# The last gathered table of 1000 rows becomes a one-hot table

## The chip, the cores and the metric

One core of one Trainium2 chip. The metric is device microseconds of one execution of the program; the median of several timed runs is given. Engines: TensorE (PE, with its weight loads shown apart as PEld), VectorE (DVE), ScalarE (ACT), GpSimd (POOL), SyncE (SP).

## What is computed

A recommendation model's interaction and top layers, for 2048 samples. Each sample has 27 ids; id f picks a row of 128 fp32 numbers from table f. Twelve tables have 1000 rows, the others 1250, 12,500 or 125,000.

```python
e = stack([tbl_f[ids[:, f]] for f in range(27)], axis=1)   # (2048, 27, 128)
inter = einsum('bfd,bgd->bfg', e, e).reshape(2048, 27 * 27)
x = inter[:, lower_triangle_without_diagonal]              # 351 pairs
h = concatenate([bottom, x, bottom], axis=1)               # (2048, 607)
h = maximum(h @ W_top1 + b_top1, 0)                        # 512
h = maximum(h @ W_top2 + b_top2, 0)                        # 256
y = h @ W_top3                                             # (2048, 1)
```

## The kernel before

The batch is worked in 8 halves of 256 samples (`HALVES`), each of two tiles of 128. Halves 0, 1 and 7 are written out, 2 to 6 are a loop on each engine. The code is written by hand for every engine, with counting semaphores.

**Two ways to a row.** `slots` divides the tables: the first `ONEHOT_TABLES` (11) with 1000 rows are one-hot, the other 16 are gathered; the slots of the gathered ones come first. A gathered table is fetched by `gather` on GpSimd: one indirect DMA (line 393) per slot and tile of 128 samples, 32 in a half, into `rows`. The rows are transposed on TensorE by `transpose_tile` (line 740), four slots to a PSUM bank: `TQ` = 4 such uses per tile, `FQ` = 4 slots each. ScalarE copies the bank into `embT` (`emb_tile`, line 548). Before a half overwrites `rows`, GpSimd waits until TensorE has transposed those of the half before.

A one-hot table lies in SBUF whole, as a high part (fp32 rounded to fp32r) and a low part (the rest), in 8 blocks of 125 rows (`VB`, `VP`). For 256 samples VectorE builds, for each block, a matrix of 125 x 256 that is 1 where the row is the sample's id (`make_hot`, line 433), and TensorE multiplies each block's high and low part with it and sums all 16 products in one bank (`onehot_unit`, line 728). Two tables share a unit and a bank; the matmuls of a table are 125x256, the hot matrices of a unit 125x512. With 11 tables there are six units, and the last has one table. A unit has four parts (two blocks each); VectorE may be four parts ahead of TensorE (`HOT_SLOTS`). It makes a part when the slot's last user is through. ScalarE copies a finished unit out (`emb_hot`, line 541).

**The order.** TensorE and ScalarE follow one list:

```python
plan = ([("hot", 0), ("hot", 1), ("tile", 0, 0), ("hot", 2), ("tile", 0, 1), ("hot", 3), ("tile", 0, 2), ("hot", 4),
         ("tile", 0, 3), ("hot", 5)] + [("tile", 1, u) for u in range(TQ)])
```

The two build banks (`ps_build`) serve units 0, 2, 4 and 1, 3, 5 in turn, then the row uses of tile 1: its first waits for the copy of unit 4, its second for the copy of unit 5. Behind the first two uses of tile 1 stand the pair products of tile 0 (`pair_products`, line 754: 64 products of two samples each, recorded as 128 matmuls of 52 columns), then the dense layers of the half before (lines 774, 802, 810) with the last two row uses between, then the pair products of tile 1. The products go by DVE and ACT copies to `gram`, to DRAM and back as `pairX`, whose 351 pair rows feed the next half's first layer. The last half multiplies per sample (line 766), and rearranges its pairs with transposes on TensorE (lines 821, 832) in the tail.

**Tables in the first half.** SP loads each one-hot table (500 KB) into one of five raw slots (`RAWS`, `load_table`); from the sixth on it waits until VectorE has made the low part of the table five before. ScalarE makes the high part (`split_table`, line 522), VectorE the low part (line 408). VectorE's order in the first half is, for each unit: its four hot parts, then the low parts of its tables. TensorE starts a unit when these are there. ScalarE's order is written out by hand: high parts of the next tables stand between its copies; `load_weights` (1.74 MB from ScalarE's queue) stands behind table 9. Behind the last table SP issues the first bottom rows and the ids of the next half.

Of the kernel before, what the change touches and what calls it, by code (L numbers as in the profile page):

```python
# [3 lines left out]

BATCH, FEATURES, D = 2048, 27, 128
SMALL_VOCAB = 1000
ONEHOT_TABLES = 11
HALF, TILE = 256, 128
HALVES = BATCH // HALF
FIRST, LAST = 0, HALVES - 1  # L10
# [17 lines left out]
def slots(vocabs):  # L28

    onehot = [f for f in range(FEATURES) if vocabs[f] == SMALL_VOCAB][:ONEHOT_TABLES]  # L30
    gathered = [f for f in range(FEATURES) if f not in onehot]
# [25 lines left out]
def dlrm_tower(nc, bottom, ids, ids_onehot, tables, w_bottom_a, w_pairs, w_bottom_b, b1, w2, b2, w3, scratch, out):  # L57
# [10 lines left out]
    TQ = (NG + FQ - 1) // FQ  # L68
# [19 lines left out]
    def bank_slots(u):  # L88

        return range(u * FQ, min((u + 1) * FQ, NG))  # L90

    def nth(*use):
        return plan.index(use)
# [46 lines left out]
    with ctx:  # L140
        def sb(name, shape, dt):
            return ctx.enter_context(nc.sbuf_tensor(name, shape, dt))
# [42 lines left out]
        ident = sb("ident", [128, 128], fp32)  # L185
# [65 lines left out]
        def build_at(s):  # L251
            return (ps_build + gram_banks)[banks[s]]
# [259 lines left out]
        def _(act):  # L512
# [7 lines left out]
            def split_table(q):  # L520
                act.wait_ge(raw_in[q % RAWS], 32 * (q // RAWS + 1))
                nc.scalar.copy(table[0:VP, q, HIGH, :], raw[0:VP, q % RAWS, :]).then_inc(table_high, 1)
# [12 lines left out]
            def emb_hot(i, p):  # L535
                s = nth("hot", p)
                act.wait_ge(built, BUILDS * i + s + 1)
                n = len(units[p])
                src = build_at(s)[:, 0:n * HALF].rearrange("p (q b) -> p b q", q=n)
                f = NG + units[p][0]  # L540
                nc.scalar.copy(embT[:, :, f:f + n], src).then_inc(emb_done, 1)  # L541

            def emb_tile(i, t, u):
                s = nth("tile", t, u)
                n = len(bank_slots(u))
                act.wait_ge(built, BUILDS * i + s + 1)
                src = build_at(s)[:, 0:n * 128].rearrange("p (f b) -> p b f", f=n)
                nc.scalar.copy(embT[:, t * TILE:(t + 1) * TILE, u * FQ:u * FQ + n], src).then_inc(emb_done, 1)  # L548
# [103 lines left out]
            emb_hot(FIRST, 3)  # L652
            emb_tile(FIRST, 0, 2)
            split_table(10)
            emb_hot(FIRST, 4)
            emb_tile(FIRST, 0, 3)
            emb_hot(FIRST, 5)
# [24 lines left out]
        def _(pe):  # L682
# [32 lines left out]
            def onehot_unit(i, n):  # L715

                s = nth("hot", n)
                bank = build_bank(i, s)
                for a in parts_of(n):
                    v0 = parts[a][1]  # L720
                    if is_half(i, FIRST) and v0 == 0:
                        pe.wait_ge(table_low, units[n][-1] + 1)
                    pe.wait_ge(hot_made, HOTS * i + a + 1)
                    for q in range(len(units[n])):
                        for v in range(VS):
                            row = (v0 + v) * D
                            for bits in (HIGH, LOW):
                                last = nc.tensor.matmul(bank[:, q * HALF:(q + 1) * HALF],  # L728
                                                        table[0:VP, units[n][q], bits, row:row + D],
                                                        hot[0:VP, a % HOT_SLOTS, v, q, :],  # L730
                                                        start=(v0 == v == q == bits == 0),
                                                        stop=(v0 == VB - VS and v == VS - 1 and bits == LOW),
                                                        skip_group_check=True)
                    last.then_inc(built if ends_unit(a) else hot_used, 1)

            def transpose_tile(i, t, u):
                pe.wait_ge(rows_in[t][u], 16 * len(bank_slots(u)) * (i + 1))
                bank = build_bank(i, nth("tile", t, u))
                for f, s in enumerate(bank_slots(u)):
                    last = nc.tensor.transpose(bank[:, f * 128:(f + 1) * 128], rows[:, t, s * D:(s + 1) * D], ident[:, :])  # L740
                last.then_inc(built, 1)
# [94 lines left out]
            def features(i):  # L836
                for use in plan[0:BUILDS - TQ + EARLY]:
                    if use[0] == "hot":
                        onehot_unit(i, use[1])
                    else:  # L840
                        transpose_tile(i, use[1], use[2])

            def first_tile(i):
                if is_half(i, LAST):
                    end_products(0)
                else:
                    pair_products(i, 0)
# [27 lines left out]
                second_tile(i)  # L875

            pe.wait_ge(consts_made, 3)
            features(FIRST)
            first_tile(FIRST)
            second_rows(FIRST)  # L880
# [61 lines left out]
```

## Time and profile before

| | us |
|---|---|
| timed runs, median of 3 | 408.24 (406.95 to 410.33) |
| profiled execution, span from first to last instruction | 600.9 |
| PE, matmuls busy in it | 416.6 |
| POOL busy | 253.9 |
| DVE busy | 198.2 |
| ACT busy | 143.3 |

For the profiled execution the profile gives only its span. The profiled execution is far longer than the timed runs, so a reader should not take shares of the span for shares of the timed run, and should look for where the extra time sits. Busy times of matmuls overlap: the distance from one start to the next is what a stream of them costs. The mean granted clock of TensorE in the execution is 0.835 of full speed.

### The profile page before, as it was taken

How to read it: one execution, taken by the hardware profiler on the slowest of the kernel's cores; microseconds unless marked ns; L12 is line 12 of the kernel's file. 1: busy time of each engine (PE TensorE's matmuls, PEld its weight loads, DVE VectorE, ACT ScalarE, POOL GpSimd, SP SyncE). 2: the span in 40 equal slices, each digit the busy share in tenths (PEclk: the TensorE clock that was granted, in tenths of full speed). 3: DMA queues.
4: the chain of work that ended last, by engine and by line, in shares of the span. 5: the costliest groups of instructions: out<-in, count | busy, mean ns of one | idle time of the engine just before them, and what ended most of it. 6: DMA issues, size and time to landing. Idle time of an engine off the chain costs nothing.

```text
span 600.9 us, 11581 instructions
## 1 busy us (share of the span) xinstructions
PE 416.6 (69%) x4550; PEld 378.3 (63%) x4550; DVE 198.2 (33%) x523; ACT 143.3 (24%) x256; POOL 253.9 (42%) x263
## 2 busy tenths in 40 slices
PE   0444655786498836897298955899378972979888
PEld 0434644676388836697186944788276962979766
DVE  3405612265204612074013722065022730138111
ACT  2302321124031221224022230322122230312423
POOL 6773563256440671526622563406723365220000
PEclk9975887698597976999579985989578995889989
DMA  7964721236112461144312461124311362122000
GB/s 161 236 146 108 191 60 52 59 76 107 36 50 54 94 104 42 36 81 92 84 36 53 88 108 31 52 59 93 96 41 31 95 92 70 41 59 52 11 2 1
DMA packets 50590, 44.79 MB, mean 75 GB/s; under 512 B 30211, under 2 KB 43019, under 8 KB 50562
## 3 DMA queue, kind: packets, MB, share of 16 engines
q1 hardware_dynamic: 40746, 25.82, 22.2%
q0 software_dynamic: 8192, 16.79, 10.8%
q10 hardware_dynamic: 1623, 1.79, 1.2%
q8 instruction: 19, 0.31, 0.2%
q14 instruction: 10, 0.07, 0.0%
HBM read 39.52 MB, written 4.85 MB: 74 GB/s over the span
## 4 chain that ended last, share of the span: by engine, by line
PE 63%; issue 23%; another core or an unknown queue 5%; DVE 4%; ACT 2%; DMA 1%; SPq 1%; ACTq 0%; DVEq 0%
PE ps_build L728 26%; PE ps_gram L754 16%; PE ps_dense L774 8%; PE ps_dense L802 4%; PE ps_build L740 3%; DVE hot L433 2%; PE ps_gram L740 2%; DMA raw<-tbl_dram 1%; PE ps_dense L810 1%; PE ps_gram L774 1%; DVE table L408 1%; ACT embT L541 1%; PE ps_gram L766 1%; PE ps_gram L821 1%
## 5 line engine op out<-in xcount | busy, mean ns | idle before, releaser
L393 POOL DMA_INDIRECT rows<-tbl_dram,idx x256 | 253.1, 989 | 275.6 <-PE ps_gram L740 96.2
L728 PE MATMUL ps_build<-hot,table 125*128 125x256 f32 x1408 | 196.3, 299 | 60.1 <-DVE table L408 34.0
L728 PEld LDWEIGHTS ps_build<-hot,table 125*128 125x128 f32 x1408 | 184.9, 204 | 65.6 <-issue 53.8
L754 PE MATMUL ps_gram<-embT 128*53 128x52 f32 x1792 | 99.5, 254 | 107.2 <-issue 106.5
L754 PEld LDWEIGHTS ps_gram<-embT 128*53 128x53 f32 x1792 | 80.8, 166 | 127.9 <-issue 125.4
L433 DVE TENSOR_SCALAR hot<-id_raw 125x512 fp32r<-125x512 f32 (+1 forms) x384 | 133.8, 408 | 76.4 <-remote 33.3
L446 DVE COPY gram<-ps_gram 117x416 f32<-117x416 f32 x28 | 16.6, 592 | 229.8 <-remote 151.1
L541 ACT COPY embT<-ps_build 128x512 f32<-128x512 f32 (+1 forms) x48 | 37.7, 786 | 176.9 <-PE ps_build L728 82.8
L559 ACT COPY gram<-ps_gram 117x416 f32<-117x416 f32 x28 | 14.2, 506 | 178.7 <-PE ps_gram L754 130.1
L774 PE MATMUL ps_dense<-pairT,w1p 120*128 120x256 f32 (+1 forms) x252 | 37.1, 295 | 0.0
L774 PEld LDWEIGHTS ps_dense<-pairT,w1p 120*128 120x128 f32 (+1 forms) x252 | 34.9, 206 | 0.0
L740 PE MATMUL ps_build<-ident,rows 128*128 128x128 f32 x128 | 20.4, 286 | 8.8 <-issue 6.9
L802 PE MATMUL ps_dense<-h,w2s 128*128 128x256 f32 x112 | 25.3, 379 | 0.0
L423 DVE TENSOR_SCALAR id_raw<-id_raw,vocab 125x512 f32<-125x512 int32 (+1 forms) x48 | 22.2, 462 | 6.2 <-DMA id_raw<-ids_onehot_dram 6.2
L548 ACT COPY embT<-ps_build 128x512 f32<-128x512 f32 x32 | 21.4, 669 | 7.4 <-PE ps_build L740 4.9
L548 ACT COPY embT<-ps_gram 128x512 f32<-128x512 f32 x32 | 21.6, 675 | 4.2 <-DVE w1b L408 2.2
L740 PEld LDWEIGHTS ps_build<-ident,rows 128*128 128x128 f32 x128 | 15.4, 146 | 11.4 <-issue 10.6
L802 PEld LDWEIGHTS ps_dense<-h,w2s 128*128 128x128 f32 x112 | 20.8, 190 | 2.6
L579 ACT ACTIVATE h<-ps_dense,b1s 128x256 f32<-128x256 f32 x28 | 13.3, 473 | 30.6 <-PE ps_dense L774 30.6
L408 DVE TENSOR_TENSOR pairT<-pairX,pairT 120x256 fp32r<-120x256 f32 (+1 forms) x21 | 7.7, 421 | 36.0 <-issue 18.9
L740 PE MATMUL ps_gram<-ident,rows 128*128 128x128 f32 x128 | 19.3, 272 | 0.0
L774 PE MATMUL ps_dense<-botT,w1b 128*128 128x256 f32 x84 | 17.6, 323 | 0.0
(57 smaller groups left out, 147.6 us busy)
## 6 DMA issues: line engine op xcount, KB each, us to landing
id_raw<-ids_onehot_dram SPq DMA_DIRECT2D x40, 256.0 KB
raw<-tbl_dram SPq DMA_DIRECT2D x11, 448.0 KB
gram_dram<-gram SPq DMA_DIRECT2D x56, 84.5 KB
rows<-tbl_dram,idx POOLq DMA_INDIRECT x256
id_raw<-ids_onehot_dram SPq DMA_DIRECT2D x8, 128.0 KB
bot<-bottom_dram SPq DMA_DIRECT2D x8, 128.0 KB
w1p_raw<-w_pairs_dram ACTq DMA_DIRECT2D x1, 720.0 KB
raw<-tbl_dram SPq DMA_DIRECT2D x11, 52.0 KB
```

What stands on the lines that cost most here:

```text
L393: nc.gpsimd.indirect_dma_start(rows[:, t, s * D:(s + 1) * D], None, tables[f], bass.IndirectOffsetOnAxis(idx[:, 2 * i + t, f:f + 1], 0)).t ...
L423: nc.vector.tensor_scalar(shifted, id_raw[0:VP, n % ID_SLOTS, 0:w, :], vocab[0:VP, 0:1], None, ALU.subtract).then_inc(id_shifted, 1)
L433: last = nc.vector.tensor_scalar(hot[0:VP, a % HOT_SLOTS, v, 0:w, :], shifted, float(v0 + v), None, ALU.is_equal)
L446: nc.vector.tensor_copy(*gram_piece(t, 2 * n + 0)).then_inc(gram_dve, 1)
L541: nc.scalar.copy(embT[:, :, f:f + n], src).then_inc(emb_done, 1)
L548: nc.scalar.copy(embT[:, t * TILE:(t + 1) * TILE, u * FQ:u * FQ + n], src).then_inc(emb_done, 1)
L559: nc.scalar.copy(*gram_piece(t, 2 * n + 1)).then_inc(gram_act, 1)
L728: last = nc.tensor.matmul(bank[:, q * HALF:(q + 1) * HALF], table[0:VP, units[n][q], bits, row:row + D], hot[0:VP, a % HOT_SLOTS, v, q, :] ...
L740: last = nc.tensor.transpose(bank[:, f * 128:(f + 1) * 128], rows[:, t, s * D:(s + 1) * D], ident[:, :])
L754: last = nc.tensor.matmul(gram_banks[b][STRIP * q:STRIP * q + GM - STRIP, g * DUO * PG:(g + 1) * DUO * PG], x.rearrange("p k g -> p (k g)" ...
L774: last = nc.tensor.matmul(bank, w(a), x(b), start=(first and m == 0), stop=(end and m == 2))
L802: last = nc.tensor.matmul(bank[:, 0:HALF], w2s[:, c, cols], h1[:, c, :], start=(c == 0), stop=(c == M1 - 1))
```

## The change

`ONEHOT_TABLES` becomes 12. So the twelfth table of 1000 rows is loaded and split like the other eleven, unit 5 has two tables, and 15 tables are gathered: the fourth row use of each tile has three slots. Sizes that follow from the numbers of tables (`NG`, `NO`: the rows, the resident tables, the ids loaded for unit 5) change with them, and SP's loop over tables has one load more, which waits for table 6's low part. ScalarE splits table 11 behind table 10. As the fourth bank of the products is now filled to column 384 only by the transposes, TensorE writes its last 128 columns once, at the start.

```diff
-ONEHOT_TABLES = 11
+ONEHOT_TABLES = 12
...
             emb_tile(FIRST, 0, 2)
             split_table(10)
+            split_table(11)
             emb_hot(FIRST, 4)
...
             pe.wait_ge(consts_made, 3)
+
+            short = TQ - 1
+            nc.tensor.transpose(build_at(nth("tile", 0, short))[:, len(bank_slots(short)) * 128:512], ident[:, :], ident[:, :])
             features(FIRST)
```

## Rows read from the trace of the kernel before

**Rows 1.** The page, part 1: busy time, share of span, instructions.

```profile
PE 416.6 (69%) x4550; PEld 378.3 (63%) x4550; DVE 198.2 (33%) x523; ACT 143.3 (24%) x256; POOL 253.9 (42%) x263
```

**Rows 2.** Windows: length, busy (x) of PE/PEld/DVE/ACT/POOL, clock, DMA share, GB/s.

```profile
324.53:351.70 27.17, 24.88 (x203) 23.88 (x200) 17.32 (x50) 8.39 (x13) 11.50 (x12) 1.00 0.45 89
351.70:374.00 22.30, 9.28 (x129) 6.95 (x128) 2.89 (x7) 2.21 (x6) 11.97 (x13) 0.57 0.31 64
...
580.95:600.90 19.95, 16.99 (x106) 14.35 (x106) 3.55 (x18) 6.16 (x23) 0.00 (x0) 0.84 0.00 1
```

**Rows 3.** Groups by line and shape: count | busy, mean ns | idle before.

```profile
L728 PE MATMUL ps_build<-hot,table 125*128 125x256 f32 x1408 | 196.3, 299 | 60.1 <-DVE table L408 34.0 <-issue 17.1 <-DVE hot L433 7.6
...
L754 PE MATMUL ps_gram<-embT 128*53 128x52 f32 x1792 | 99.5, 254 | 107.2 <-issue 106.5 <-ACT embT L548 0.7
L541 ACT COPY embT<-ps_build 128x512 f32<-128x512 f32 x40 | 32.4, 811 | 163.3 <-PE ps_build L728 76.9 <-remote 52.3 <-PE ps_gram L740 24.4
...
L541 ACT COPY embT<-ps_build 128x256 f32<-128x256 f32 x8 | 5.3, 665 | 13.6 <-PE ps_build L728 5.9 <-PE ps_build L740 4.3 <-remote 3.4
L766 PE MATMUL ps_gram<-embT 128*26 128x26 f32 x512 | 5.1, 192 | 4.6 <-issue 4.6
```

**Rows 4.** PE in order of time, a middle half: start, us, what, idle before.

```profile
337.20 0.60 PE L740 MATMUL ps_gram<-ident,rows 128*128 128x128 f32 x4
337.56 4.08 PE L728 MATMUL ps_build<-hot,table 125*128 125x256 f32 x32
341.47 0.60 PE L740 MATMUL ps_gram<-ident,rows 128*128 128x128 f32 x4
...
347.56 2.15 PE L728 MATMUL ps_build<-hot,table 125*128 125x256 f32 x16
...
379.47 0.52 PE L774 MATMUL ps_dense<-botT,w1b 128*128 128x256 f32 x3
...
380.91 3.62 PE L802 MATMUL ps_dense<-h,w2s 128*128 128x256 f32 x16
384.36 0.60 PE L740 MATMUL ps_build<-ident,rows 128*128 128x128 f32 x4
384.89 1.02 PE L810 MATMUL ps_dense<-h,w3s 128*1 128x256 f32 x4
...
391.68 2.38 PE L754 MATMUL ps_gram<-embT 128*53 128x52 f32 x61 [0.46 <-issue]
393.99 0.58 PE L728 MATMUL ps_build<-hot,table 125*128 125x256 f32 x1
...
559.05 0.63 PE L740 MATMUL ps_build<-ident,rows 128*128 128x128 f32 x4 [0.41 <-ACT embT L541]
```

**Rows 5.** POOL in order of time, the same half.

```profile
334.54 1.10 POOL L393 DMA_INDIRECT rows<-tbl_dram,idx  x1 [12.73 <-PE ps_gram L740]
...
366.38 0.94 POOL L393 DMA_INDIRECT rows<-tbl_dram,idx  x1 [0.30 <-issue]
```

**Rows 6.** The first half: the chain's DMA, then PE and DVE in order of time.

```profile
5.04 9.00 DMA raw<-tbl_dram
...
16.47 5.80 PE L728 MATMUL ps_build<-hot,table 125*128 125x256 f32 x32 [16.47 <-DVE table L408]
...
70.03 5.55 PE L728 MATMUL ps_build<-hot,table 125*128 125x256 f32 x32 [2.73 <-issue]
...
77.35 2.14 PE L728 MATMUL ps_build<-hot,table 125*128 125x256 f32 x16 [1.33 <-ACT embT L548]
...
59.66 0.76 DVE L433 TENSOR_SCALAR hot<-id_raw 125x512 fp32r<-125x512 f32 x2 [0.19 <-PE ps_build L728]
60.34 2.35 DVE L408 TENSOR_TENSOR table<-raw,table 125x1024 fp32r<-125x1024 f32 x2
...
75.62 0.49 DVE L433 TENSOR_SCALAR hot<-id_raw 125x256 fp32r<-125x256 f32 x2 [0.86 <-PE ps_build L728]
76.03 1.22 DVE L408 TENSOR_TENSOR table<-raw,table 125x1024 fp32r<-125x1024 f32 x1
```

## The prediction

> **What bounds the kernel now.** I began with the page: TensorE (PE) is the busiest engine, 416.6 us in a span of 600.9 us [rows 1]. But the span of the profiled execution is 192.7 us above the median of the timed runs, 408.24 us, and its matmul busy time alone is above that median. So the profiled execution holds time that a timed run does not, and shares of its span say little. Where is it? The windows of one half in the middle of the loop show it: its one-hot stage lasts 27.17 us with PE busy for 24.88, and the pair products behind it last 22.30 us with PE busy for 9.28 [rows 2]. The group of the pair products puts its idle time down to "issue", 106.5 us in all, so it waits for nothing that the profile names. In a stretch where the same matmuls run freely, 61 of them start within 2.31 us (391.68 to 393.99), 0.0379 us each, and the 128 of a stage would take 4.9 us instead of 22.3 [rows 3, 4].
>
> So I rebuilt a timed run from start-to-start spacings in undisturbed stretches [rows 4], times the counts [rows 3]:
> - one-hot matmuls: 32 between 337.56 and the transposes at 341.47, 3.91 us; 1408 of them are 44 such sets, 172.0 us;
> - pair products: 1792 x 0.0379 = 67.9 us;
> - transposes: 4 from 337.20 to 337.56, 0.36 us; 256 are 23.0 us;
> - first dense layer: 12 from 379.47 to 380.91, 1.44 us; it has 48 matmuls per half, so 46.1 us over 8 halves. The second layer: 3.45 us per half (380.91 to 384.36), 27.6 us; the third, busy 1.02 us per half, 8.2 us.
>
> That is 344.8 us. The last half's own products are 5.1 us [rows 3], and its tail keeps PE busy for 16.99 us, 10.2 of them its dense layers, which are in the sum: 6.8 more [rows 2]. The first matmul starts at 16.47 us [rows 6]. Together 373.2 us, out of 408.2. The 35.0 us left are waits: in the first half PE stands before each further one-hot unit for its tables' splits, 2.73 us before unit 4 [rows 6], which for five units makes 13.7 us; in the tail 3.0 us of 19.95 [rows 2]; and 18.3 us remain for eight halves, 2.3 us each. A middle half is 5.5 x 3.91 + 8 x 0.36 + 256 x 0.0379 + 5.76 + 3.45 + 1.02 = 44.3 us of matmuls, about 46.6 us with such waits. **PE's throughput sets the end**, nearly without slack.
>
> POOL is the second candidate. A gather is busy 0.94 us behind a gap of 0.30 (366.38), so the 32 of a half take 39.7 us; beside the hot building one is busy 1.10 us (334.54), and 8 such make it 41.0 us [rows 5]. That is 3 us under PE's 44.3 us, and the first gather of a half is preceded by 12.73 us of waiting for PE's transposes (less in a timed run, whose pair products don't stall, but by the sums some 3 us more than nothing). POOL waits for PE.
>
> **The change part by part.**
>
> *Added: 16 matmuls in unit 5 of each half.* Unit 5 has 16 now, busy 2.15 us (347.56); the full unit at 337.56 is busy 4.08 us. Added: 1.93 us per half [rows 4]. They are in PE's only stream, nothing lies beside them. The lower bound is nothing (all of it in waits that PE has today), the upper is the lower clock, by unit 4 of the first half: 5.55 us for 32, 2.8 us for 16 [rows 6]. I take 1.93. The Trainium skill (TensorE: Matmul & The Clock Gate, Back-to-back issue gap and LDWEIGHTS) has two rules here: an isolated matmul of N columns every N/2.4 + 2.5 ns, 109 ns for 256 columns, and a weight load of 107 ns for 128 columns. The 122 ns of a pair in the trace [rows 4] fit a weight load that is hidden and a small cost above the first rule; if the load were not hidden the 128 added pairs would cost 27.6 us, by the first rule alone 14.0 us, by the trace 15.4 us.
>
> *Removed: 2 transposes per half* (the fourth row use of either tile has three slots): 2 x 0.09 = 0.18 us per half, from PE's stream [rows 4].
>
> *Removed: 2 gathers per half on POOL*, 2.5 us of its queue [rows 5]. Worth nothing, as POOL waits for PE; the bounds are 0 and -2.5 us.
>
> *ScalarE.* The copy of unit 5 out of PSUM goes from 128x256, 665 ns, to 128x512, 811 ns: +0.15 us [rows 3]. This one is on the path: the second of the two early transposes writes unit 5's bank, and PE stands 0.41 us before it for this copy (line 541) at 559.05 [rows 4]. I add 0.15 per half. The two copies of the short tiles get narrower; I take nothing for them (at most 0.1 us each).
>
> *VectorE.* A part of unit 5 is two instructions, 0.49 us together for one table (75.62) and 0.76 us for two (59.66) [rows 6]: four parts make +1.1 us per half. VectorE is busy for 17.32 us of the 27.17 of the one-hot stage, so this is hidden [rows 2]. The cover is the four hot slots: a part of unit 5 will need 1.0 us of PE and 0.76 us of VectorE [rows 4, 6]. Without that cover it would be the 1.1 us per half.
>
> A half thus costs 1.93 - 0.18 + 0.15 = +1.90 us, seven halves +13.3 us.
>
> *The first half* is limited otherwise. VectorE makes a unit's last hot part only when PE has freed a slot, and splits the unit's tables behind it. So PE stands still for 2.73 us before unit 4. Before unit 5 the chain is: last hot part 75.62, split 76.03 (1.22 us), PE 77.35 [rows 6]. With two tables the hot part is 0.27 us longer and the splits take 2.35 us, as at 60.34, instead of 1.22: +1.13. So PE starts 1.40 us later, then has 1.93 us more, less 0.18, plus 0.15: **+3.3 us**. At the slower clock that unit 4 shows (5.55 us busy instead of 4.08) the added matmuls are 0.9 us more.
>
> The twelfth table must also land. It is the seventh load that waits for a raw slot, the one of table 6, which is free when its low part is made, at about 61.5 (the first of the two splits of 60.34 to 62.69). A table that was on the path took 9.00 us from issue to landing among a full load [rows 6]: 70.5. ScalarE must split it before its copy of unit 4, due at 75.6. Its split takes about as long as VectorE's, 1.2 us. That leaves 4 us of cover, some 2.5 us if unit 4 runs at full clock, and the weights (1.74 MB) are issued at the same time. I take nothing, and keep +4 us as the upper bound. SP's next loads (the bottom rows and three sets of ids of the next half) stand behind its new wait for the slot; they are wanted a half later, tens of us. The first gathers get 2 fewer and the ids of unit 5 twice 128 KB, both small.
>
> *The one new transpose at the start* runs when the identity is made, in PE's 16.47 us without work: nothing.
>
> Sum: 13.3 + 3.3 = 16.6 us. The durations are those of the profiled execution, its undisturbed stretches; against its own span, 600.9 us, the same sum gives 617.5 us. On the median of the timed runs it is 408.24 + 16.6 = **424.8 us**, 4.1% more.
>
> **The rivals.**
>
> *The added matmuls fill waits that PE has anyway.* For it: some 18 us of the 408 remain as waits by my sum, and the fractions per half (0.41 us before the second early transpose) may be larger than I see. Against: the added matmuls are in unit 5, where PE's stream in the trace has no wait, and hots or gathered rows come no earlier by the change. Then only the first half grows: 411.5 us. Chance 0.07.
>
> *POOL sets the pace, and loses 2 of its 32 gathers.* This is the case on the other side. If a gather took 46.6/32 = 1.46 us in a timed run, POOL would fill the whole half and PE would wait for rows at its transposes. After the change 30 gathers take 43.7 us. Whether that shows depends on PE: from a stream of 44.3 + 1.9 = 46.2 us PE takes over at once, and the time is 408.24 - 7 x 0.4 + 3.3 = 409 us. It decides for a gain where PE's own stream is at least 2.5 us per half shorter than my sum of it; then a half falls by 2.9 us, and 408.24 - 7 x 2.9 + 3.3 = 391 us. For it: gathers beside hot building take 1.40 us with the gap. Against: only 8 of 32 do, the rest 1.24 us, and PE releases the first [rows 5]. The Trainium skill (DMA: Bandwidth & Descriptors, SWDGE vs HWDGE vs iDMA) says that VectorE, in its two-port mode, locks GpSimd out of the memory its descriptors go to; that would raise just these. Chance 0.03 for 409 us and 0.03 for 391 us.
>
> *The twelfth table lands late*, behind the weights: +4 us on top, 428.8 us. Chance 0.10.
>
> *The added matmuls run at 1.2 GHz everywhere.* 8 x 0.9 us more: 432 us. The granted clock was 1.00 over the one-hot stage of the half [rows 2], so I give it 0.03.
>
> **How the numbers follow.** The forecast, 424.8 us with its own range 419 to 428, has 0.73; 0.01 is left for what I do not see. The range: 415 us (half of the addition is absorbed) to 430 us (a late table). The first two rivals and the clock lie outside it, 0.16 together. A difference of 1% is about what a measurement of this kernel can tell from none. Faster by over 1%: POOL's second case with what I do not see, 0.04. Within 1% (404.2 to 412.3): the absorbed case and POOL's first, 0.10. Slower: the rest, 0.86.
>
> **What would show it.** Right: 1536 one-hot matmuls at the same mean; 240 gathers and 240 transposes of rows; unit 5 as long as the others, 3.9 us; the one-hot stage of a middle half some 1.9 us longer and the other stages as before; the first half's unit 5 starting 1.4 us later after unit 4, and 3.3 us more up to the pair products; POOL's wait before a half's first gather longer by some 4 us. Wrong: PE waiting for rows before a transpose, ScalarE waiting for the load of the last table, or PE waiting for hots in unit 5. If the timed runs do not rise by 10 us though unit 5 does grow by 1.9 us, then my reconstruction of the timed run as bound by PE is the step that failed.

## The result and the profile after

| | median us | before, beside it | ratio, 95% interval |
|---|---|---|---|
| changed kernel, first measurement | 418.34 | 407.6 | 1.0315 (1.0263 to 1.0366) |
| again (e5) | 424.64 | 408.81 | 1.0461 (1.0384 to 1.0539) |
| again (e12) | 425.33 | 407.19 | 1.0345 (1.0275 to 1.0414) |

The change makes the kernel 3 to 5% slower. The ratios are of the fast runs of both kernels, so they are not exactly the quotients of the medians. One more thing has to be known to read what follows: the kernel before has two levels of time by the chip it runs on, near 408 us and, on one chip met here, near 601 us, in its timed runs as in its profile. By its span and its stages the profile shown of before is of the second kind, the timed runs are of the first. So I took the kernel before again on a chip of the first kind (e9 below), and compare with that.

The page of the changed kernel, part 1, answers to [rows 1]:

```profile
PE 365.7 (88%) x4663; PEld 347.0 (83%) x4663; DVE 213.5 (51%) x524; ACT 141.7 (34%) x257; POOL 250.4 (60%) x247
```

Its windows (columns as in [rows 2]), from the first one-hot matmul to the first pair products, from there to half 1, then half 1, half 2, and two middle halves:

```profile
17.21:68.24 51.03, 35.85 (x216) 34.43 (x216) 30.20 (x55) 17.12 (x21) 38.41 (x36) 0.83 0.92 212
68.24:76.64 8.40, 7.55 (x264) 7.20 (x264) 4.27 (x10) 3.28 (x6) 6.56 (x7) 1.00 0.35 92
76.64:125.45 48.81, 45.58 (x550) 43.31 (x547) 26.95 (x66) 17.92 (x31) 37.84 (x36) 0.97 0.53 107
125.45:171.97 46.52, 44.16 (x550) 41.93 (x547) 24.46 (x63) 15.70 (x29) 30.96 (x31) 1.00 0.55 103
171.97:216.65 44.68, 43.90 (x549) 41.83 (x547) 24.36 (x63) 15.72 (x29) 29.04 (x30) 1.00 0.50 103
216.65:261.32 44.67, 43.89 (x550) 41.82 (x547) 24.43 (x63) 15.68 (x29) 30.75 (x31) 1.00 0.48 106
```

The same stages of the kernel before (e9):

```profile
0.00:65.67 65.67, 35.53 (x201) 34.14 (x201) 33.18 (x66) 19.46 (x23) 49.30 (x53) 0.84 0.86 197
65.67:74.19 8.52, 7.66 (x265) 7.31 (x265) 4.43 (x10) 3.40 (x6) 6.69 (x7) 1.00 0.37 100
74.19:118.74 44.55, 42.37 (x537) 40.17 (x533) 26.26 (x66) 17.93 (x31) 34.48 (x34) 1.00 0.46 109
118.74:169.60 50.86, 43.88 (x536) 41.57 (x533) 23.09 (x63) 15.90 (x29) 38.96 (x40) 0.93 0.52 104
169.60:212.48 42.88, 42.19 (x532) 40.13 (x533) 22.92 (x63) 15.84 (x29) 29.32 (x30) 1.00 0.51 106
212.48:255.36 42.88, 42.19 (x536) 40.13 (x533) 23.14 (x63) 15.87 (x29) 31.82 (x33) 1.00 0.58 110
```

A middle half goes from 42.88 to 44.67 us, with PE busy for 98% of it in both. The rest is unlike. The table gives what each stage is longer than in e9, in the profile of the first measurement and in that of e5:

| us longer than in e9 | first measurement | e5 |
|---|---|---|
| up to the first pair products | 2.6 | 4.9 |
| from there to half 1 | -0.1 | -0.1 |
| half 1 | 4.3 | 2.4 |
| half 2 | -4.3 | -6.2 |
| halves 3 to 6 | 7.2 | 7.1 |
| half 7 and the tail | 0.0 | 4.7 |
| whole span | 9.6 | 12.8 |

Only halves 3 to 6 are alike. Halves 1 and 2 hold stalls of PE that the profile puts down to "issue" (in e9 6.27 us in half 2; in the first measurement 2.36 and 1.58, in e5 2.02 in half 1 alone), of which more below. A stall costs more than its own length. In e9 the granted clock was 0.73 in the 6.07 us behind it, which by that clock are some 1.6 us too long (an estimate, 6.07 x 0.27). Without the two, e9's half 2 is a middle half like the others, 42.95 us:

```profile
148.66:154.93 6.27, 0.00 (x1) 0.00 (x0) 0.47 (x2) 0.00 (x0) 4.75 (x6) 0.71 0.99 183
154.93:161.00 6.07, 6.07 (x39) 5.96 (x39) 0.00 (x0) 2.08 (x4) 4.69 (x5) 0.73 0.28 74
```

In half 1 part of the added work fills a wait that PE had before. There PE stands before the second early transposes for ScalarE's copies, and ScalarE for the splits of the weights on VectorE. The wait is 1.57 us in e9 and 0.52 in the changed kernel:

```profile
99.97 0.63 PE L740 MATMUL ps_build<-ident,rows 128*128 128x128 f32 x4 [1.57 <-ACT embT L541]
```

```profile
103.13 0.63 PE L741 MATMUL ps_build<-ident,rows 128*128 128x128 f32 x4 [0.52 <-ACT embT L541]
```

So without its stall of 2.02 us, e5's half 1 is only 0.4 us longer than e9's (44.94 against 44.55). In half 7 and the tail the granted clock differs from one execution to the next: from the transposes of the last pairs to the end it was 0.92 in e9 (18.8 us), 1.00 in the first measurement (17.4 us) and 0.86 in e5 (20.0 us).

Where do the 1.79 us sit? PE in order of time, the end of one middle half's one-hot stage and the later row uses, changed kernel:

```profile
237.85 0.49 PE L741 MATMUL ps_gram<-ident,rows 128*128 128x128 f32 x3
238.10 4.08 PE L729 MATMUL ps_build<-hot,table 125*128 125x256 f32 x32
242.01 0.60 PE L741 MATMUL ps_build<-ident,rows 128*128 128x128 f32 x4
243.04 0.66 PE L741 MATMUL ps_build<-ident,rows 128*128 128x128 f32 x4 [0.42 <-ACT embT L541]
243.62 3.36 PE L755 MATMUL ps_gram<-embT 128*53 128x52 f32 x128
246.91 0.62 PE L775 MATMUL ps_dense<-botT,w1b 128*128 128x256 f32 x3
```

The same in e9:

```profile
233.69 0.60 PE L740 MATMUL ps_gram<-ident,rows 128*128 128x128 f32 x4
234.05 2.15 PE L728 MATMUL ps_build<-hot,table 125*128 125x256 f32 x16
236.04 0.60 PE L740 MATMUL ps_build<-ident,rows 128*128 128x128 f32 x4
236.96 0.66 PE L740 MATMUL ps_build<-ident,rows 128*128 128x128 f32 x4 [0.32 <-ACT embT L541]
237.55 3.36 PE L754 MATMUL ps_gram<-embT 128*53 128x52 f32 x128
240.83 0.62 PE L774 MATMUL ps_dense<-botT,w1b 128*128 128x256 f32 x3
```

Unit 5 takes 3.91 us instead of 1.99 (+1.92); the short tile's transposes 0.25 instead of 0.36, twice (-0.22); the wait for unit 5's copy 0.42 instead of 0.32 (+0.10). The sum is +1.80. And the pair products start every 0.0257 us (3.29 us for 128), not every 0.0379 as I had read in [rows 4]. The stretch that I had read it in was not undisturbed: its granted clock was 0.67, and 0.0257 is 0.68 of 0.0379.

```profile
391.68:393.99 2.31, 2.31 (x62) 2.22 (x62) 1.34 (x4) 0.51 (x1) 0.00 (x0) 0.67 0.01 4
```

### The profile page after: what moved, and what is told of

It is laid out like the page before. It is cut to its first block, busy times and chain, and to the rows that moved or that the text cites. A ratio compares the mean times of both kernels' runs of the same rounds, so it can differ in the third digit from the quotient of the medians.

```text
span 415.8 us, 11801 instructions
## 1 busy us (share of the span) xinstructions
PE 365.7 (88%) x4663; PEld 347.0 (83%) x4663; DVE 213.5 (51%) x524; ACT 141.7 (34%) x257; POOL 250.4 (60%) x247
## 3 DMA queue, kind: packets, MB, share of 16 engines
q10 hardware_dynamic: 1623, 1.79, 1.9%
## 4 chain that ended last, share of the span: by engine, by line
PE 80%; issue 5%; DMA 5%; ACT 4%; DVE 3%; ACTq 1%; SPq 1%; DVEq 0%
PE ps_build L729 42%; PE ps_gram L755 11%; PE ps_dense L775 10%; PE ps_dense L803 6%; DMA raw<-tbl_dram 5%; PE ps_gram L741 3%; PE ps_build L741 3%; ACT embT L541 2%; PE ps_dense L811 2%; PE ps_gram L775 1%; ACTq L518 1%; DVE hot L433 1%; PE ps_gram L767 1%; DVE table L408 1%; PE ps_build L803 1%
## 5 line engine op out<-in xcount | busy, mean ns | idle before, releaser
L729 PE MATMUL ps_build<-hot,table 125*128 125x256 f32 x1536 | 204.7, 293 | 32.3 <-DVE table L408 18.2
L729 PEld LDWEIGHTS ps_build<-hot,table 125*128 125x128 f32 x1536 | 195.6, 200 | 35.5 <-DVE table L408 18.7
L433 DVE TENSOR_SCALAR hot<-id_raw 125x512 fp32r<-125x512 f32 x384 | 148.0, 443 | 23.0 <-PE ps_build L729 16.9
L541 ACT COPY embT<-ps_build 128x512 f32<-128x512 f32 x48 | 38.7, 807 | 146.5 <-PE ps_build L729 143.5
L755 PEld LDWEIGHTS ps_gram<-embT 128*53 128x53 f32 x1792 | 45.3, 129 | 6.6 <-issue 3.9
L755 PE MATMUL ps_gram<-embT 128*53 128x52 f32 x1792 | 47.2, 213 | 2.4 <-issue 1.6
L423 DVE TENSOR_SCALAR id_raw<-id_raw,vocab 125x512 f32<-125x512 int32 x48 | 23.0, 480 | 6.6 <-DMA id_raw<-ids_onehot_dram 6.6
L741 PE MATMUL ps_build<-ident,rows 128*128 128x128 f32 x120 | 18.8, 276 | 6.0 <-ACT embT L541 3.7
L548 ACT COPY embT<-ps_build 128x512 f32<-128x512 f32 (+1 forms) x32 | 20.1, 632 | 4.7 <-PE ps_build L741 4.6
L548 ACT COPY embT<-ps_gram 128x512 f32<-128x512 f32 (+1 forms) x32 | 20.7, 647 | 2.3 <-DVE w1b L408 2.3
L522 ACT CAST table<-raw 125x1024 fp32r<-125x1024 f32 x12 | 12.5, 1048 | 24.1 <-DMA raw<-tbl_dram 24.1
```

The costliest lines, as they stand in the source:

```text
L423: nc.vector.tensor_scalar(shifted, id_raw[0:VP, n % ID_SLOTS, 0:w, :], vocab[0:VP, 0:1], None, ALU.subtract).then_inc(id_shifted, 1)
L433: last = nc.vector.tensor_scalar(hot[0:VP, a % HOT_SLOTS, v, 0:w, :], shifted, float(v0 + v), None, ALU.is_equal)
L729: last = nc.tensor.matmul(bank[:, q * HALF:(q + 1) * HALF], table[0:VP, units[n][q], bits, row:row + D], hot[0:VP, a % HOT_SLOTS, v, q, :] ...
L755: last = nc.tensor.matmul(gram_banks[b][STRIP * q:STRIP * q + GM - STRIP, g * DUO * PG:(g + 1) * DUO * PG], x.rearrange("p k g -> p (k g)" ...
```

## The experiments

Four sets, each on one chip. Ratios are to the kernel before in the same set.

**e1, e9: the kernel before, unchanged.**

> The kernel before, unchanged, for a profile in which the pair products do not stall. My theory (TensorE sets the end): a span of 400 to 408 us, a middle half of 42.7 us (the 44.67 us of the changed kernel less 1.9), no wait for rows, the pair products of a tile in 3.3 us. Rival (GpSimd sets the pace before the change and hid part of what was added): a middle half of over 43.2 us, or waits of TensorE before transposes in some halves that the changed kernel does not have, 4 to 5 us in all. Second rival (the first half costs less than I forecast): a middle half of 42.7 us and a first half up to the pair products under 2 us shorter than the changed kernel's 68.24 us.

The chip of the first set was of the 601 us level: 604.5 us (before in that set: 601.51, 11 runs). So the long stages of [rows 2] are no effect of being profiled. Windows there, in a first pair-product stage: while gathers run, from the last gather's end to PE's return, and after:

```profile
363.91:376.55 12.64, 3.59 (x41) 2.28 (x40) 1.09 (x3) 2.21 (x5) 9.59 (x11) 0.53 0.35 84
376.55:379.53 2.98, 0.81 (x3) 0.50 (x4) 0.00 (x0) 0.00 (x0) 0.00 (x1) 0.50 0.09 22
379.53:383.51 3.98, 3.98 (x85) 3.87 (x84) 1.80 (x4) 0.51 (x1) 0.00 (x0) 0.50 0.00 0
```

41 matmuls in 12.6 us with the gathers, 85 in 4.0 us behind them, at granted clocks of 0.53 and 0.50: it is not the clock that tells these two stretches apart.

> The kernel before, unchanged, once more for a profile, hoped for on a chip of the 408 us level. There: middle halves of 42.88 us (as in the runs without later gathers and with the splits first, both with this kernel's TensorE work), against 44.67 of the changed kernel; so the other 4 us of the 16.6 that I forecast and that were not measured lie elsewhere. Theory I: in the first turn of the loop TensorE stands for 4 to 6 us with nothing to wait for (code that it runs for the first time), where the changed kernel stands for 0 to 2. Rival F: the first half is not 3.3 us shorter than the changed kernel's but as long. On a chip of the 601 us level this run is a repetition.

Ratio 0.997 (0.9908 to 1.0032), middle halves of 42.88 us, as expected; the way to the first pair products is 2.6 us shorter than the changed kernel's, so rival F is not it either. The stall in the first turn of the loop is there:

```profile
154.93 0.37 PE L774 MATMUL ps_dense<-pairT,w1p 120*128 120x256 f32 x1 [6.27 <-issue]
```

**e2: the changed kernel without the twelfth table's matmuls**

```diff
-                    for q in range(len(units[n])):
+                    for q in range(1 if n == len(units) - 1 else len(units[n])):
```

> The changed kernel, in which TensorE leaves out the 16 matmuls per half of the twelfth table (so its embeddings are not computed); all loads, splits, hot matrices, copies and the 15 gathers stay. If TensorE sets the end, it is faster than the changed kernel by 8 x 1.93 to 2.2 us, 15.4 to 17.6 us, so near 402 us, and the rest of the change (402 against 407.6) is a gain of some 5 us. If the added matmuls cost less than I sized, near 407 us.

**e3: the kernel before with 14 gathers fewer**

```diff
                     for s in bank_slots(u):
+                        if i > 0 and s == NG - 1:
+                            continue
...
```

The other lines of this edit let TensorE wait for the smaller number of rows.

> The kernel before, in which the last gathered slot is fetched in the first half only, so GpSimd has 30 gathers in each further half and the rows of that slot are stale from then on. TensorE does the same work as before. My theory in the prediction (gathers removed are worth nothing): ratio to before 1.00 within 0.3%. Rival (GpSimd had a part in the time before): 4 to 5 us faster, ratio 0.99.

**e4: the changed kernel with two gathers per half put back**

```diff
...
+                if 2 * i + t > 0:
+                    pool.wait_ge(spare_in, 16 * (2 * i + t))
+                f = onehot[-1]
+                nc.gpsimd.indirect_dma_start(
+                    spare[:, :], None, tables[f],
+                    bass.IndirectOffsetOnAxis(idx[:, 2 * i + t, f:f + 1], 0)).then_inc(spare_in, 16)
```

> The changed kernel with two more gathers per half again, of the twelfth table's rows into a spare buffer that nobody reads, one behind the gathers of each tile. If gathers are worth nothing: 418.3 us, as the changed kernel. Rival (GpSimd had a part): 2 to 5 us slower than that, 420 to 423 us, with GpSimd's wait before a half's first gather shorter by 2.5 us.

All three ran on the 601 us chip, for which none of the expected numbers had been made. The ratios: e2 0.941 (0.9358 to 0.9462), e3 0.955 (0.9495 to 0.9605), e4 1.0099 (1.0046 to 1.0153). The starts of unit 0 give the middle halves, one of four shown of each. e3:

```profile
307.14 6.01 PE L730 MATMUL ps_build<-hot,table 125*128 125x256 f32 x48
371.99 6.01 PE L730 MATMUL ps_build<-hot,table 125*128 125x256 f32 x48
```

e1 and then e4:

```profile
333.67 6.19 PE L728 MATMUL ps_build<-hot,table 125*128 125x256 f32 x48
403.46 7.00 PE L728 MATMUL ps_build<-hot,table 125*128 125x256 f32 x48
```

```profile
326.47 6.85 PE L737 MATMUL ps_build<-hot,table 125*128 125x256 f32 x48
396.49 6.08 PE L737 MATMUL ps_build<-hot,table 125*128 125x256 f32 x48
```

69.8 us with 32 gathers, 64.9 with 30, and 70.0 with 32 gathers and 16 more matmuls; on average over the four middle halves 69.6, 65.0 and 69.8, and 65.0 in e2. On that chip the gathers set a middle half's length and the matmuls hide in it: there my "a gather is worth nothing" is wrong by some 2.3 us each. The whole of e4 is still 1% over the kernel before; where that sits was not looked into. The changed kernel itself did not come to a chip of that level. It has e2's gathers (567.3 us) and up to 15.4 us of matmuls more, so I expect under 583 us, a gain of 3% or more; that is an estimate.

**e5, e12: the changed kernel again.** Ratios in the table above.

> The changed kernel, unchanged. The first four runs showed that the kernel before has two levels of time, near 408 us and near 601 us, by the chip. Where the kernel before is near 408 us: 1.03 of it, as measured. Where it is near 601 us (there TensorE issues almost nothing in the pair products while gathers run): theory G, gathers set the end there and each of the 14 that go in halves 1 to 7 is worth 2 us, as in the run without them (28 us), while the added matmuls cost about 15 us: 0.975 to 0.985 of the kernel before, so the change is a gain there. Rival P, the added matmuls cost what they cost on the other chip and gathers are hidden behind them: 1.01 to 1.03 there too.

> The changed kernel once more, on whichever chip comes. On one of the 408 us level: two ratios are known, 1.0315 and 1.046, and my sum is 1.041. If TensorE's stalls on new code (2 to 9 us in all by the profiles, at the same places in the code, of other lengths in each run) are what scatters, this ratio lies between them, 1.03 to 1.046, and the profile has middle halves of 44.67 us again. On one of the 601 us level: by theory G a gain, ratio 0.965 to 0.985, as this kernel without its added matmuls was at 0.941 and with two more gathers per half at 1.010; by theory P 1.01 to 1.03.

e5 came to 1.0461, and the 1.03 that I expected is outside its interval. e12 came to 1.0345, between the two as expected, with middle halves of 44.67 to 44.70 us.

**e6: the added matmuls alone**, in the kernel before; the second product goes into the unread half of the bank.

```diff
-                    for q in range(len(units[n])):
+                    for q in range(2):
+                        w = min(q, len(units[n]) - 1)
...
-                                                        table[0:VP, units[n][q], bits, row:row + D],
-                                                        hot[0:VP, a % HOT_SLOTS, v, q, :],
+                                                        table[0:VP, units[n][w], bits, row:row + D],
+                                                        hot[0:VP, a % HOT_SLOTS, v, w, :],
```

> The kernel before, in which the last one-hot unit multiplies its one table twice, the second time into the unread half of its bank: TensorE has the change's 16 more matmuls per half, and nothing else is changed. TensorE sets the end: 8 x 1.93 us = 15.4 us slower, on a chip near 408 us: ratio 1.038. Rival (before the change TensorE had waits that they fill): under 10 us. On a chip near 601 us by theory G the added matmuls stand ahead of the stage that waits for the gathers, and part of them is hidden: 5 to 15 us.

421.43 us, ratio 1.0309 (1.0239 to 1.0378), 12.6 us; the forecast 1.038 is just outside the interval. So most of the change's cost comes with these matmuls alone, but the timed runs of e6 and of the changed kernel (1.0461 in the same set) do not tell the two apart finely enough to price the rest. The profile does, for a middle half: 44.79 us in e6, 1.91 over e9, and the changed kernel's 44.67 is 0.12 less.

```profile
176.31:221.10 44.79, 44.11 (x548) 42.04 (x549) 22.87 (x63) 15.87 (x29) 27.92 (x30) 1.00 0.44 100
```

**e7: no gathers after the first half** (rows of halves 1 to 7 stale)

```diff
-            for i in range(1, HALVES):
-                for t in range(2):
-                    gather(i, t)
...
```

> The kernel before with the gathers of halves 1 to 7 left out (the rows are those of the first half throughout). TensorE has all its work. Theory G: the long pair-product stages vanish on any chip, the middle half is 42.7 us, and the time is near 400 us, on a chip where the kernel before takes 408 us and on one where it takes 601 us; a middle half's first pair products take 3.3 us instead of 22.3. Rival S (the stall is TensorE's instruction supply or its records whatever else runs): still near 550 to 600 us on such a chip.

On a chip of the 408 us level: 406.35 us, not near 400, and a ratio of 0.9942 (0.9893 to 0.9992), with the same middle half. Unit 1's second part in two of them:

```profile
217.15 2.18 PE L725 MATMUL ps_build<-hot,table 125*128 125x256 f32 x16 [0.37 <-DVE hot L430]
260.03 2.18 PE L725 MATMUL ps_build<-hot,table 125*128 125x256 f32 x16 [0.37 <-DVE hot L430]
```

42.88 us, as with 32 gathers. There all 224 gathers together are worth 0.6%, at most about 1%, and none of it in a middle half. The stall in the first turn of the loop is there without gathers too, 4.61 us of it. Theory G was not tested where it would matter, on the other chip.

**e8, e11: the splits ahead of the hot parts**, in the kernel before and in the changed one.

```diff
             for n, unit in enumerate(units):
+                for q in unit if n else ():
+                    split_table(q)
                 for a in parts_of(n):
                     make_hot(FIRST, a)
-                for q in unit:
+                for q in () if n else unit:
                     split_table(q)
```

> The kernel before, in which VectorE splits a unit's tables ahead of its hot parts in the first half (but for unit 0), so that the splits run beside the matmuls of the unit before. The chain that I priced at 2.73 us before each unit goes: if it bounds the first half, 5 x 2.4 = 12 us faster. Rival (the loads bound it; the DMA engines are full up to 50 us): 0 to 5 us faster.

> The changed kernel with VectorE's splits ahead of the hot parts in the first half. The kernel before gained 1.6% by it (a first half 9 us shorter). With twelve tables the last unit has two tables to split, so the gain is the same or a little larger: 8 to 11 us under the changed kernel, 407 to 410 us on a chip of the 408 us level, so at the level of the kernel before and some 12 us above that kernel with the splits first. Rival: the full load of twelve tables bounds the first half, and the gain is under 6 us.

e8: 399.61 us, ratio 0.9845 (0.9782 to 0.9908). It beats both kernels, by less than the 12 us that I expected if the splits bound the first half. Up to the pair products:

```profile
0.00:55.67 55.67, 30.92 (x200) 29.56 (x200) 32.81 (x66) 19.70 (x23) 41.94 (x44) 0.94 0.97 217
```

10.0 us earlier than e9's 65.67, with the DMA engines full (share 0.97). e11: 416.38 us, ratio 1.0205 (1.0148 to 1.0261), pair products from 58.43, and a total that is 3.7% over e8's (1.0205/0.9845): with a shorter first half the change costs what it cost before, 14.7 us. The 407 to 410 us that I expected were missed by 6 us or more, though the pair products did begin 10 to 12 us earlier than in the changed kernel; in this profile the stalls of halves 1 and 2, given below, are 8.8 us, and unit 5 stood for 3.78 us.

**e10: TensorE's code shifted**, by 57 transposes before the first unit.

```diff
             pe.wait_ge(consts_made, 3)
+            for n in range(57):
+                nc.tensor.transpose(build_at(nth("tile", 0, 0))[:, 0:128], ident[:, :], ident[:, :])
```

> The kernel before with 57 transposes of the identity at the start, in TensorE's idle time before the first table; they move all later TensorE code by as many instructions as the change does up to the loop. Theory I: the stall of TensorE in the first turn of the loop (4 to 6 us in kernels with 11 tables) shrinks to 0 to 2 us as in the changed kernel, and the time falls by 2 to 5 us; middle halves stay at 42.88 us. If the place of the code has no bearing: the stall stays, ratio 1.00. A side effect: unit 0 may run at the full clock, which could give another 1 to 2 us in the first half; the stall is read from the trace by itself.

405.07 us, ratio 0.986 (0.98 to 0.9919). The time fell, but not for the reason of theory I: in the profile the stall was not gone, but had moved from half 2 to half 1:

```profile
110.11 0.80 PE L774 MATMUL ps_dense<-botT,w1b 128*128 128x256 f32 x3 [6.54 <-issue]
```

So its place hangs on where the code lies. Its length does not only: the changed kernel had 2.36 us in half 1 and 1.58 in half 2, then 2.02 and none (e5), 3.67 and none (e12), and with the splits first, at the same two places, more:

```profile
104.42 0.47 PE L743 MATMUL ps_build<-ident,rows 128*128 128x128 f32 x1 [3.78 <-issue]
...
152.33 1.68 PE L757 MATMUL ps_gram<-embT 128*53 128x52 f32 x31 [4.98 <-issue]
```

Against 6.3 us in e9 and 8.4 in e6. The traces show what ends these stalls. Beside the data the DMA queues carry packets of the kind "instruction". The queues in e9's stall, 148.66 to 154.93 us (packets, MB, share of the 16 engines):

```profile
q1 hardware_dynamic: 463, 0.62, 73.7%
q0 software_dynamic: 243, 0.51, 24.2%
q8 instruction: 1, 0.02, 0.9%
```

Queue q8 carries 19 or 20 packets of 16 KB in a whole execution. They come while TensorE runs code for the first time, and none comes in halves 3 to 6, where it repeats the loop. In e9's stall the packet begins at 152.41 us and takes 0.91, and PE goes on 1.6 us later. The same holds for all twelve stalls of over 1 us in halves 1 and 2 of the nine profiles of the 408 us level: each ends 1.3 to 1.6 us after such a packet has landed. The profile does not name the engine that a packet is for, but that TensorE waited for its own code is what fits all twelve. At most of the other such packets TensorE did not stall (e5 has the packet of half 2 at 151.82 us and no stall); why one comes late is not shown. Whether twelve tables stall less than eleven is not settled either, nor is the 1.4% of e10 explained: its profiled execution has the same stall and a span of 405.5 us, 0.7 us under e9's.

## Why the prediction was right, and where it was off

The forecast was 424.8 us against 408.24, a ratio of 1.041; three measurements gave 1.0315, 1.0461 and 1.0345, on average 15 us instead of 16.6. The reason holds too: TensorE's throughput sets the end on a chip of the 408 us level. e6 shows it (only matmuls added, 1.91 us per middle half) and e7 (no later gathers, the same middle half). That the total came so near is in part luck, as errors in both directions met.

- *The profiled execution holds time that a timed run does not.* Right for those timed runs, but being profiled is not the reason: by its span the profile came from a chip on which a timed run takes that long too. To rebuild the time from undisturbed stretches was the right use of it.
- *A middle half has 44.3 us of matmuls, some 46.6 with waits.* It has 42.88 in all. The mis-sized term is the pair products, 0.0379 us read in a stretch of 61 at a granted clock of 0.67, 0.0257 measured at 1.00: 3.1 us too much for 256. So the sum of 373.2 us is some 22 us too high for the 1792 pair products, and the waits, low clocks and stalls outside the middle halves are as much larger than the 35.0 us that I gave them.
- *POOL waits for PE.* It does, but by less than I said: e9's POOL waits 1.61 us before a half's first gather, where a half of 46.6 us would have left over 5. In the changed kernel it is 5.07 us, 3.5 us more; I had forecast some 4. The first line is e9, the second the changed kernel, each in half 4:

```profile
222.48 1.12 POOL L393 DMA_INDIRECT rows<-tbl_dram,idx  x1 [1.61 <-PE ps_gram L740]
```

```profile
226.44 1.31 POOL L393 DMA_INDIRECT rows<-tbl_dram,idx  x1 [5.07 <-PE ps_gram L741]
```

  So the rival on the other side was nearer than its 0.06: 1.6 us more of gathers per half and PE would wait. Gathers beside the hot building again took longer, 1.08 to 1.12 us against 0.94 in e9; here they cost nothing. The Trainium skill (DMA: Bandwidth & Descriptors, SWDGE vs HWDGE vs iDMA) would lead one to expect it, as VectorE in its two-port mode locks GpSimd out of the memory that holds the descriptors; no run here shows that this is the reason.
- *Per half +1.93, -0.18, +0.15.* Measured in a middle half +1.92, -0.22, +0.10: 1.80 instead of 1.90. I took it for seven halves. It holds for halves 3 to 6, and half 1 took only 0.4 of it (in e5, without its stall): there my rival of waits that the added matmuls fill was right. VectorE's longer parts are hidden, as forecast: the one wait for hots stays at 0.36 us.
- *The first half, +3.3 us.* From unit 4's start to the pair products e9 takes 11.0 us (54.66 to 65.67), the changed kernel 17.0 (51.26 to 68.24) and in e5 16.8 (53.77 to 70.58): +5.8 to +6.0. The term that failed is unit 5's own, 1.93 us. The second split lengthens PE's pause before it from 1.47 to 2.9 us, and behind that pause the granted clock was low. Windows over unit 5 in the changed kernel:

```profile
60.08:66.56 6.48, 6.48 (x33) 6.48 (x34) 0.00 (x0) 0.00 (x0) 4.96 (x6) 0.55 0.38 74
```

  and in e6, with the same 32 matmuls behind a pause of 1.37 us:

```profile
60.08:63.99 3.91, 3.91 (x32) 3.91 (x33) 0.00 (x0) 0.00 (x0) 3.00 (x4) 1.00 0.32 98
```

  6.48 against 3.91 us, mostly at 1.2 instead of 2.4 GHz (0.55 against 1.00). I had that as an upper bound, 0.9 us, and for the 16 added matmuls alone; it met all 32 and is 2.6 us (1.3 in e5, at 0.72, where unit 4 lost another 1.2 to a low clock). In all eight profiles in which the pause before unit 5 was 1.3 to 1.7 us, unit 5 ran at full speed, and in all six in which it was 2.8 to 3.8 us it did not. It is not a rule for every pause: unit 1 of the changed kernel, behind 3.12 us, ran at 1.00:

```profile
26.33:30.26 3.93, 3.93 (x32) 3.93 (x33) 2.68 (x7) 1.88 (x2) 3.02 (x4) 1.00 1.06 241
```

  In e9 unit 1 was at 0.56 and took 6.62 us. This is why the change costs only 2.6 us up to the pair products in that profile, and 4.9 in e5.
- *The twelfth table lands in time.* Right: ScalarE made the high parts of tables 10 and 11 in one go, with no wait for a DMA (at 49.44 us, 2.00 us for two).
- *The new transpose at the start costs nothing.* Right, it ran at 1.64 us.
- *Not in the forecast:* stalls of TensorE on code that it runs for the first time, 2 to 9 us in halves 1 and 2, which vary from execution to execution. They are as large as the gap between two measurements of this change. In the profiles shown, e9's one stall with the low clock behind it is what makes its half 2 longer by 4.3 us than the changed kernel's, though that has 1.80 us more to do: 6.1 us of the cost are hidden by it.

So in the first profile the change costs 9.6 us: 2.6 in front, 4.3 in half 1, -4.3 in half 2, 7.2 in halves 3 to 6, nothing in half 7 with the tail. The 7.2 us are the forecast mechanism, at its forecast size. The 3.3 us of the first half were too small by 2.5 us for unit 4 and what follows it, half 1 hid over 1 us, and the rest is stalls and granted clocks, which differ in each execution. One profile for each kernel cannot divide the 12.8 us of the first measurement (0.0315 x 407.6) further.

## What to carry to other kernels

When a profile's span is far from the timed runs, look whether it belongs to the same level of machine before anything is taken from it, and read spacings only in stretches with no stall near and at a granted clock of 1.00. Where one engine is busy for 98% of a loop turn, work moved onto it costs its full length, and work taken from the next engine is worth nothing until that one is the bound; here GpSimd was 1.6 us away from it. A pause that grows can cost twice: by itself, and by the clock of what comes behind it. And one profile for each of two kernels can hide half of a change in a stall that only one of the executions had.

## What was not expected of the hardware

The same program takes 408 us on three chips (and in the first runs) and 601 us on a fourth, and the difference lies where indirect DMAs run beside TensorE's smallest matmuls: 22.3 us for 128 of them instead of 3.3 [rows 2]. PE is put down as waiting for "issue" there, and is back at speed some 3 us after the last gather. Taking 2 of 32 gathers away shortened a middle half by 4.6 us on average (69.6 to 65.0), nearly twice their 2.5 us on GpSimd. It is not the loading of code, with which the stalls of the first turns go. The queues in the stage of 22.3 us, 351.70 to 374.00 us of the profile of before, show no packet of the kind "instruction":

```profile
q0 software_dynamic: 512, 1.05, 16.5%
q1 hardware_dynamic: 403, 0.38, 14.7%
```

and in that whole profile queue q8 has none from 250.2 to 540.2 us, while each half between has its long stage. What else in the chip holds TensorE's issue there I did not find.
